# A fused token, attention and mixture-of-experts kernel: the order of its shared-expert units, the PSUM banks they use, and where its expert weights are split

## What is computed

```
h = concat(tok(x), txt)                              # (8, 384, 512)
h = h + attn(layernorm(h))                           # latent 128 -> 64, rope, causal softmax
h = h + ffn(layernorm(h))
# ffn, per token row n:
scores = softmax(n @ gate_weight.T)                  # 8 experts in 4 groups; 2 groups, then 2 experts are kept
routed = sum_e w_e * (silu(n @ gate_e.T) * (n @ up_e.T)) @ down_e.T      # 352 hidden features per expert
shared = (silu(n @ sh_gate.T) * (n @ sh_up.T)) @ sh_down.T               # 704 hidden features, every token
```

## Time and profile before

| | us |
|---|---|
| median of three runs | 974.26 |
| lowest, highest | 972.4, 977.86 |
| the profiled execution | 966.46 |
| its span | 964.6 |
| TensorE busy in it | 829.0 |
| VectorE, ScalarE, GpSimd busy in it | 513.3, 395.0, 349.4 |

### The profile page before, as it was taken

One profiled execution on the slowest core, in us unless ns is written; L12 is line 12 of the kernel. 1 busy time (PEld: TensorE's weight loads), 2 busy tenths in 40 slices (PEclk: granted clock), 3 DMA queues, 4 the chain that ended last, 5 costly groups with the idle time before them and its releaser, 6 DMA issues.

```text
span 964.6 us, 20136 instructions
## 1 busy us (share of the span) xinstructions
PE 829.0 (86%) x7301; PEld 522.5 (54%) x7302; DVE 513.3 (53%) x919; ACT 395.0 (41%) x683; POOL 349.4 (36%) x352
## 2 busy tenths in 40 slices
PE   0009999989799999699859997999999999999993
PEld 0009997655355545355436553666666666666661
DVE  7997746656652544736776442455434444444441
ACT  5863324334223232537442153454444444444441
POOL 0056744413810011524331032344444444444442
PEclk9999999989989999999979998999999999999996
DMA  5021234044412003597342054354444544444542
GB/s 191 0 66 47 59 111 143 24 88 121 111 45 66 1 24 108 135 225 160 92 90 80 23 153 155 79 89 83 83 79 85 87 87 76 79 85 86 87 76 33
DMA packets 66046, 84.68 MB, mean 88 GB/s; under 512 B 36096, under 2 KB 36224, under 8 KB 65344
## 3 DMA queue, kind: packets, MB, share of 16 engines
q0 software_dynamic: 12480, 29.37, 17.4%
q1 hardware_dynamic: 41408, 31.48, 11.8%
q10 hardware_dynamic: 12096, 22.94, 8.7%
HBM read 48.38 MB, written 27.53 MB: 79 GB/s over the span
## 4 chain that ended last, share of the span: by engine, by line
PE 72%; DVE 12%; ACT 6%; POOL 3%; issue 3%; DMA 2%; ACTq 0%; DVEq 0%; POOLq 0%
PE PS L2087 10%; PE PS L2089 10%; PE PS L2088 10%; PE PS L1075 7%; PE PS L590 6%; PE PS L1076 6%; PE PS L1077 6%; PE PS L2097 3%; PE PS L746 2%; PE PS L2119 2%; PE PS L1276 2%; PE PS L1233 1%; PE PS L2028 1%; DVE work L1422 1%; PE PS L1234 1%
## 5 line engine op out<-in xcount | busy, mean ns | idle before, releaser
L2087 PE MATMUL PS<-big,work 128*128 x605 | 200.9, 332 | 4.1 <-ACT work L2165 2.4
L2089 PE MATMUL PS<-big,work 128*128 x605 | 201.2, 333 | 0.0
L2088 PE MATMUL PS<-big,work 128*128 x605 | 201.2, 332 | 0.0
L2274 POOL DMA_INDIRECT out_dram<-work x55 | 88.0, 1600 | 62.5 <-DVE work L2244 46.0
L2206 DVE SCALAR_TENSOR_TENSOR work<-work,PS 128x352 f32<-128x352 f32 x55 | 28.7, 522 | 154.0 <-PE PS L2089 154.0
L2165 ACT ACTIVATE work<-PS 128x1024 f16<-128x1024 f16 x55 | 56.3, 1024 | 85.2 <-PE PS L2097 85.2
L2087 PEld LDWEIGHTS PS<-big,work 128*128 128x128 f16 x605 | 59.3, 98 | 42.6 <-issue 6.7
L2089 PEld LDWEIGHTS PS<-big,work 128*128 128x128 f16 x605 | 59.4, 98 | 42.2 <-issue 0.3
L2088 PEld LDWEIGHTS PS<-big,work 128*128 128x128 f16 x605 | 59.2, 98 | 36.5 <-issue 0.3
L994 POOL TENSOR_TENSOR big<-work,big 128x544 f16<-128x544 f32 (+1 forms) x30 | 38.0, 1267 | 108.8 <-ACT work L980 108.8
L2261 POOL DMA_INDIRECT big<-x_dram,work x55 | 55.8, 1015 | 46.7 <-POOL work L2258 45.0
(11 more groups left out here) (284 smaller groups left out, 1754.2 us busy)
## 6 DMA issues: line engine op xcount, KB each, us to landing
work<-in_weights ACTq DMA_DIRECT2D x36, 272.0 KB, 2.8
work<-in_shared ACTq DMA_DIRECT2D x28, 256.0 KB, 3.3
x_dram<-big SPq DMA_DIRECT2D x24, 256.0 KB, 2.3
out_dram<-big SPq DMA_DIRECT2D x24, 256.0 KB, 3.5
big<-in_weights ACTq DMA_DIRECT2D x20, 272.0 KB, 2.9
big<-in_weights SPq DMA_DIRECT2D x1, 2176.0 KB, 9.8
big<-in_par SPq DMA_DIRECT2D x1, 1185.0 KB, 10.7
big<-in_c_real SPq DMA_DIRECT2D x1, 1024.0 KB, 5.8
```

The costliest lines, as they stand in the source:

```text
L2087: pe.matmul(out, x_high, w_high, start=start, stop=False)
L2088: pe.matmul(out, x_high, w_low, start=False, stop=False)
L2089: return pe.matmul(out, x_low, w_high, start=False, stop=stop)
L2274: pool.indirect_dma_start(out_d, bass.IndirectOffsetOnAxis(ap=S_NUM[u][:, 0:1], axis=0), YO[u], None, compute_op=ALU.add).then_inc(s_add, 16)
```

## The change

Five things change together.

1. The order of the units is a list, `UNITS`: the first gate unit of a sequence comes ahead of the three down units of the sequence before it.
2. Units 46 to 105 use seven banks, (n - 46) % 7, once the attention is over; the others three as before. `bank_free` waits for the last unit that had the same bank.
3. All low parts are made on VectorE; `split_low_g` and the scaling on ScalarE (L980) are gone. Which piece is split at which unit comes from a table, `LATE_COUNT`: none at an up unit, one at a gate unit, two at a down unit; of an up unit, VectorE makes the low part of the piece of the unit before between the product and its low part. The first 8 late pieces are split inside the attention part. There is a seventh staging buffer (the late pieces now take five in turn, then four), and the order of the blocks changes.
4. The attention of pairs 2 and 3 stands two or three units earlier; VectorE's statistics, norms, ropes and stores are laid between units one at a time; on GpSimd the bias of pairs 2 and 3 comes after the deviations of pair 1 and waits until unit 14 is done.
5. The router's logits stand earlier, its count after unit 75 (before: 73), the first table after unit 83 (before: 79), and the eight tables are spread over 12 units (before: 16). The last piece is split at unit 109.

```diff
+UNITS = [(b, u) for b in range(B) for u in range(SH_UNITS)]
+for b in range(1, B):
+    UNITS[SH_UNITS * b - 3:SH_UNITS * b + 1] = [(b, 0)] + [(b - 1, u) for u in range(MCH, SH_UNITS)]
+def after(b, u):
+    return UNITS.index((b, u)) + 1
...
-        LATE_BLOCKS = (1, 4, 6, 5, 7, 0, 8)
+        LATE_PIECES = [(block, k) for block in (1, 6, 4, 5, 7) for k in range(PIECES)]
+        LATE_PIECES += [(8, k) for k in range(3)] + [(0, k) for k in range(PIECES)] + [(8, k) for k in range(3, PIECES)]
+        for n in range(43, B * SH_UNITS):
+            u = UNITS[n][1]
+            if n < 86:
+                count_here = 0 if u in UP_UNITS else 2 if u >= MCH else 1
+                LATE_COUNT[n] = min(count_here, LATE_PIECES.index((8, 0)) - PIECES - sum(LATE_COUNT))
+            elif n < 94:
+                LATE_COUNT[n] = int(n in (88, 90, 92))
+            else:
+                count_here = 2 if n in (97, 98) else int(n < 97 or u in (2, 4, 5, 7, 9, MCH))
+                LATE_COUNT[n] = min(count_here, len(LATE_PIECES) - PIECES - sum(LATE_COUNT))
...
             act.activation(piece_out(q, 0), stage(q), ACT.Copy, scale=W_SCALE).then_inc(sp_high, 1)
-            if q in ON_POOL:
-                act.wait_ge(sp_high, q + 1)
-                act.activation(stage(q), stage(q), ACT.Copy, scale=W_SCALE).then_inc(sp_scaled, 1)
...
-        def split_low_g(pool, q):
-            pool.wait_ge(sp_scaled, ON_POOL.index(q) + 1)
-            pool.tensor_tensor(piece_out(q, 1), stage(q), piece_out(q, 0), ALU.subtract).then_inc(sp_low_g, 1)
...
         def bank_of(n):
-            return 4 + n % 3
+            return (n - LATE_FROM) % 7 if LATE_FROM <= n < LATE_TO else 4 + n % 3
+        LATE_FROM, LATE_TO = 46, 106
...
         # attn_tensor
-            ffn_tensor(pe, 8, 14)
+            ffn_tensor(pe, 8, 11)
             pe.wait_ge(s_xt[1], 3 * 16)
             logits(pe, 1, XT_SH[1])
-            ffn_tensor(pe, 14, 18)
+            ffn_tensor(pe, 11, 18)
             q_tensor(pe, 2)
...
-            ffn_tensor(pe, 32, 34)
+            ffn_tensor(pe, 30, 32)
             q_tensor(pe, 3)
-            ffn_tensor(pe, 34, 35)
+            ffn_tensor(pe, 32, 33)
             qkv_tensor(pe, 3)
...
-            ffn_tensor(pe, 64, 74)
+            ffn_tensor(pe, 62, 76)
             count(pe)
-            ffn_tensor(pe, 74, 80)
+            ffn_tensor(pe, 76, 84)
             for q in range(TABLE_TURNS):
                 make_table(pe, q)
-                ffn_tensor(pe, 80 + 2 * q, 82 + 2 * q)
+                ffn_tensor(pe, 84 + 3 * q // 2, 84 + 3 * (q + 1) // 2)
             ffn_tensor(pe, 96, B * SH_UNITS)
...
         # attn_vector, after unit 42
-            norm_rows(dve, 18)
-            ffn_split_vector(dve, 49, 51, q + 3)
-            norm_rows(dve, 21)
-            ffn_split_vector(dve, 51, 56, q + 5)
+            norm_row(dve, 18)
+            ffn_split_vector(dve, 46, 47)
+            moments(dve, 3, "b")
+            for k in range(4):
+                norm_row(dve, 19 + k)
+                ffn_split_vector(dve, 47 + 2 * k, 49 + 2 * k)
+            norm_row(dve, 23)
...
         # attn_gpsimd
-            bias(pool, 1)
             c_scale(pool, 1, 1, 2)
             for i in range(PAIRS - 1):
                 for half in range(2):
                     deviation(pool, i, "ab"[half])
                     rows_low(pool, 6 * i + 3 * half)
-                    if i == 0 and half == 1:
-                        for q in range(MCH, SHARED_PIECES):
-                            split_low_g(pool, q)
-                        bias(pool, 2)
+                    if i == 0 and half == 0:
+                        bias(pool, 1)
                     if i == 1 and half == 1:
+                        c_scale(pool, 2, 2, PAIRS)
+                        pool.wait_ge(ff_p, SH_UNITS + 1)
+                        bias(pool, 2)
                         bias(pool, 3)
-                        c_scale(pool, 2, 2, PAIRS)
```

More of the change, by code:

```diff
@@ L910, in place @@
                 return q % 4 if q < MCH else q % 2
[L911 to L915, removed]
+            k = q - SHARED_PIECES
+            if k < PIECES:
+                return (2, 3, 1, 0)[k % 4]
+            return (2, 3, 6, 1, 0)[(k - PIECES) % 5] if k < LAST_FROM else (0, 1, 4, 5)[(k - LAST_FROM) % 4]
         def low_done(eng, q):
[L919 to L926 removed]
+            eng.wait_ge(sp_low, q + 1)
         PLACES = [place(q) for q in range(SPLITS)]
+        AHEAD = tuple(range(5, SHARED_PIECES)) + tuple(range(SHARED_PIECES + 4, SPLITS))
         def ahead(q):
[L931 removed]
+            last = max((k for k in range(q) if PLACES[k] == PLACES[q]), default=q - 5)
+            if PLACES[q] in (4, 5) and PLACES.index(PLACES[q]) == q:
+                return 1
+            return max(1, min(3, q - last - (1 if q < SHARED_PIECES else 2)))
         def stage(q):
@@ L1077, in passes @@
             return pe.matmul(out, a_low, b_high, start=False, stop=stop)
+        LATE_FROM, LATE_TO = 46, 106
+        BANKS = [bank_of(n) for n in range(B * SH_UNITS)]
         def bank_free(pe, n):
-            if n < 0:
+            earlier = [k for k in range(n) if BANKS[k] == BANKS[n]]
+            if not earlier:
+                if n >= LATE_FROM:
+                    pe.wait_ge(oa_v.sem, oa_v.at(f"h5_{PAIRS - 1}"))
+                    pe.wait_ge(at_a.sem, at_a.at(f"oT{PAIRS - 1}"))
                 return
-            b, u = divmod(n, SH_UNITS)
+            n = earlier[-1]
+            b, u = UNITS[n]
             if u >= MCH:
@@ L1169, in ffn_vector @@
                     v.scalar_tensor_tensor(x, x, KSC[r, :], PS[r, bank_of(n), 0:S], ALU.mult, ALU.mult).then_inc(ff_mul, 1)
-                    if piece is not None:
-                        split_low(dve, piece + n - n0)
+                    if late:
+                        lows(dve, n)
                     dve.wait_ge(ff_hi, g + 1)
@@ L1178, in ffn_vector @@
                     v.scalar_tensor_tensor(x, PS[:, bank_of(n), :], OSC, x, ALU.mult, ALU.add).then_inc(ff_add, 1)
-                if u not in UP_UNITS and piece is not None:
-                    split_low(dve, piece + n - n0)
-        LOGIT_ORDER = (0, 1, 2, 3, 4, 6, 7, 5)
+                if u not in UP_UNITS and late:
+                    lows(dve, n)
+        LOGIT_ORDER = (0, 1, 2, 3, 4, 6, 5, 7)
         def read_logits(dve, k):
```

335 lines of the change are left out of this document (198 added, 137 removed).

## The result

| | before | after |
|---|---|---|
| median of the runs, us (lowest to highest) | 973.33 (971.74 to 977.86, 4 runs) | 928.72 (926.82 to 931.29, 4 runs) |
| profiled execution, us | 966.46 | 927.49 |
| its span, us | 964.6 | 925.6 |

The ratio is 0.9536 with the interval [0.9494, 0.9578]. (The runs of before taken beside those of after have the median 973.33; 974.26 is that of the first three.) The time is inside the range of 928 to 960 by 0.7 us only, 12 us under the forecast of 941 and closer to the rival in which all goes (930). From trace to trace the saving is 39.0 us, from median to median 44.6.

The account below looks back on a forecast made before the run. TensorE was taken to wait for VectorE, late mainly by its order. Waits of 34.7 us and five restarts (9.5) gained, 10.4 given back, net 34, held at 33: 974.26 becomes 941 us, range 928 to 960.

Parts of the forecast that it names:

- the rival in which all goes: Whole kernel: every listed wait and restart goes and nothing is given back, 930 us; chance 0.17.
- the waits of 9.9, 9.4, 7.2, 4.5, 2.4 and 1.5 us: TensorE's waits: first table's masks, block-end low parts, banks (units 15, 16), router's selection, pair 3's attention, routed start; 34.9 us.
- The router's chain: From count to first table's masks: VectorE needs 19.5 us, TensorE's units cover 19.9; 1 us of wait left.
- That the router stays the bound: Count and first table: VectorE as late as before, so 4.5 and 9.9 us and two restarts stay, 959 us; chance 0.18.
- The loads do not set the pace at the end: Rival at the hand-over to the routed experts: last weight loads set the pace, saving covered, 970 to 975 us; chance 0.05.
- The backlog of over 5.3 us at block ends: Rival at block ends: VectorE falls behind by over 5.3 us, down units wait, 984 us; chance 0.06.
- I carry the saving over to: Whole kernel: the saving of 33 us, reckoned on the profiled execution of 966.46, applied unchanged to the median of 974.26.
- The attention part gets 8 pieces ... I take 2.: Attention part: 8 more pieces on VectorE cost between nothing and 6 us; 2 us given back.
- 2.5 us new, perhaps one restart (1.9): Eight tables over 12 units: two or three new waits of 1 to 1.5 us, 2.5 us, plus one restart of 1.9.
- 1.3 gone: Start of the routed experts: the last piece is split two units earlier, removing 1.3 of the 1.5 us wait.
- The 9.4 us at block ends: Down units waiting for last low parts: single norms, freed ScalarE and gate-unit skew remove 9.4 us and two restarts (3.8).
- Contention: Where the bias of pairs 2 and 3 runs: GpSimd slows VectorE's two-input instructions, sum 3 to 4 us worse.

Follow-up runs that it names:

- Kernel 1: Kernel before with all 46 of GpSimd's low parts made on VectorE and ScalarE's scalings gone, nothing else: 957.85 us, ratio 0.9863.
- kernel 7: Kernel after with the router's count, first table and table spacing back at their old places: 934.59 us, ratio 0.9632.
- kernel 6: Kernel after with three banks throughout, the old order of units and the last six norms in threes: 932.85 us, ratio 0.9604.
- kernel 9: Kernel after with 24 low parts around the router's steps back on GpSimd, and ScalarE's scaling for each: 936.72 us, ratio 0.9666.
- Kernel 12: Kernel before with 30 unused matmuls on TensorE ahead of the first table turn: one run, 971.75 us.
- kernel 10: Kernel after with GpSimd's bias of pair 1 ahead of the deviations again: 927.6 us, ratio 0.9569.
- kernel 11: Kernel after with pair 1's bias first again and pieces 13 and 14 split behind pair 1's additions: 922.47 us, ratio 0.9504.
- kernels 3: Kernel after with three banks throughout in place of seven for units 46 to 105: 927.12 us, ratio 0.9561.
- 5: Kernel after with the last six row norms in two groups of three: 926.26 us, ratio 0.9567.
- 8: Kernel after with GpSimd's bias of pairs 2 and 3 at its old place: 927.37 us, ratio 0.9568.
- kernels 2: Kernel before with seven banks in turn for units 46 to 105, nothing else: 969.82 us, ratio 1.0002.
- kernel 4: Kernel after with the units in the old order, each sequence's first gate unit behind its predecessor's downs: 928.62 us, ratio 0.9577.

## Why the prediction was right, and where it was off

**Right in kind.** TensorE waited for VectorE's order, not for its amount of work: the waits of 9.9, 9.4, 7.2, 4.5, 2.4 and 1.5 us of the earlier trace rows are gone or under 1 us, and the clock from 243 us to the end of the shared units is 0.99 to 1.00. The sign named for being right, 0.97 or more from 209 us on, failed in its first stretch (0.85 over 209 to 243 us). The first routed turn starts 36.7 us earlier (558.23 against 594.92; forecast some 35). The router's chain was costed at 19.5 us against 19.9 of cover; it took 19.6 us, to 473.86, and the first table started at 473.92 without a wait. That the two agree to 0.1 us is partly luck: the 19.6 hold the 1.82 us in which VectorE waited for TensorE, so its own part was 17.8. How the whole saving divides is known in part only. Kernel 1 has 13 us, kernel 7 another 7 to 8 and kernel 6 4 to 7; the other 16 to 20 (the statistics and norms laid apart, the earlier attention and logits, parts acting together) no run isolates.

**The rivals.** That the router stays the bound would have needed a chain of over 20 us; kernel 9, at 24.6, shows that rival with its wait of 5.2. The loads do not set the pace at the end; in the attention of pair 1 two of them hold VectorE up. The backlog of over 5.3 us at block ends did not come up.

**Steps that were off:**

- *"I carry the saving over to" the median.* The profiled execution of before lay 6.9 us under the median of its runs (973.33), that of after 1.2 us under its own. Of the 44.6 us between the medians, 5.6 are this difference, nearly half of the 12 us miss. Kernel 12's trace, of 971.75 us, shows what such a difference is made of: it is 5.0 us behind before's at unit (0,10), by TensorE's clock.
- *"The attention part gets 8 pieces ... I take 2."* The part up to unit (0,10) lost 6.9 us. The bounds of nothing to 6 us were drawn from VectorE's busy time alone. They left out the bias of pair 1, moved into VectorE's busy time (up to 1.9 us in the trace of kernel 10, nothing measurable in its runs), and two pieces that wait for a load with additions queued behind them (kernel 11: 2.2 us between traces, 5 between medians). Some 5 of the 6.9 us come and go from trace to trace, so the 2 us fit the better traces (1.7).
- *"2.5 us new, perhaps one restart (1.9)" at the tables.* The waits came as said, 3.3 us in three; the restart did not. Their longest is 1.4 us. With the 1 us for the first table, 2.1 us too much was given back, net.
- *The gain in the shared units.* From unit (0,10) on, the terms (33.4 us of waits, 9.5 of restarts, less 3.3 at the tables) give 39.6; measured 41.9. The 1 us for pair 2's rescale was right but does not show in this trace, in which TensorE comes late: kernels 3, 5, 8, 10 and 11 wait 1.4 us for it (L1234). Kernel 3, 5 us earlier at unit (0,10), takes 310.1 us for the same units, 40.1 gained. So 1.8 of the 2.3 us between terms and measurement belong to the early loss.
- *"1.3 gone" at the start of the routed experts.* This stage gained 4.0 us. The hand-over wait gave 1.5; another 1.7 is a slow start not counted as a restart (from the first L2097 to the second took 7.07 us, after 5.39), and 0.8 is not assigned. TensorE's first routed instructions, before and then after:

```profile
597.03 0.44 PE L2089 MATMUL PS<-big,work 128*128 x1
...
597.56 0.50 PE L2088 MATMUL PS<-big,work 128*128 x1
```

```profile
560.34 0.31 PE L2166 MATMUL PS<-big,work 128*128 x1
```

- *The 9.4 us at block ends.* The gain was right in size but was credited to the wrong parts: skew ("5.3 us in place of 3.4"), single norms and fewer scalings. Each of skew, norms and banks alone is worth nothing, all three some 4 to 7 us (kernels 2 to 6). Collisions were left out here too: the three norms of the earlier trace rows took 3.18 us beside GpSimd's work on the rows, three elsewhere 1.46, and they have only one input each.
- *Contention.* The Trainium skill (GPSIMD Engine Reference, Key points) was weighed as 3 to 4 us against the change where the bias of pairs 2 and 3 runs. The kind of effect agrees with the traces (0.56 to 1.30 us for the rope beside GpSimd), but at that place it costs nothing measurable: kernel 8, with the bias elsewhere, has the same time, and units 15 to 22 run without a wait. Where the chain is tight it costs more than was put on it: 5 us in the router's chain alone, 9 to 10 in all with ScalarE's scalings (kernel 9), and 13 us in the kernel of before for all 46 pieces with their scalings (kernel 1).

The misses partly cancel. Trace to trace 39.0 us came where 33 were forecast. The attention part lost 4.9 us more than the 2 put on it. The shared units gained 5.4 more (41.9 against 42.9 - 1 - 1 - 4.4 = 36.5), the start of the routed experts 2.7 more, and the 2.8 us for the unseen and for rounding stayed: -4.9 + 5.4 + 2.7 + 2.8 = 6.0.

## What to carry to other kernels

An engine that is idle a third of the time can still bound another one through its order. Work out for each place how long its chain is and how much work of the waiting engine covers it: that arithmetic (19.5 against 19.9) found a dead heat here, and it was one; more cover and the absence of collisions were both needed for it. Cushions such as banks and skews should be tested by removing them one by one and together, since one alone may show nothing. A stage of one trace can be 5 us off by clock and loads: look at several traces of the same program before a few us are given a cause. When work is moved out of an engine's idle time, ask which engine is busy at the new place and what stands queued behind it if its input is late: this cost 2 to 5 us here, and could be mended.

## What the runs showed of the hardware

- GpSimd beside VectorE lengthens VectorE's smallest instructions too: a scalar operation with one input on 128x8 took 1.14 us and, 1.2 us later, 0.17; one on 128x3 took 1.03 against 0.17. With two inputs: 0.95 to 1.73 (128x768), 0.50 to 1.40 (128x330), 0.56 to 1.30 and 1.51 (128x384). In these pairs the addition is 0.7 to 1.0 us whatever the instruction's size, so it is the small ones that multiply. It is not a fixed price, though. In the chains of kernel 9 and of before each long instruction begins while one of GpSimd's (1.2 to 1.7 us) runs and ends just after it or within its own short time: 455.00 to 456.14 us beside GpSimd's 454.89 to 456.11. The later it begins in GpSimd's instruction, the less is added: at 480.02 us in before, beside GpSimd's to 480.68, 0.87 us in place of 0.36. Not all instructions are touched: a product that reads PSUM took 0.61 us beside GpSimd at 465.24 in kernel 9, as without it.
- The length of a single wait does not settle whether half clock follows. Waits of TensorE of 0.8 to 1.4 us at the tables were not followed by it; one of 3.2 us was, and so was one of 1.08 us at L1276 in kernel 12, behind 19 us at clock 1.00 (then 0.50 over 235 to 240 us). In before the same wait, of 1.09 us, was followed by it some 2.5 us later; in kernel 3 one of 0.73 us at this place was not. Between these lies the 2.4 us wait at L1223 of before, behind which no slow unit was seen. But before, the first routed tile was slow behind two waits close together, 1.5 us at L2097 and 1.2 at L2087; after, behind the 1.2 us alone, it was not.
